# A fused transformer block on one core: mixing weights spread as 8 tokens by 16 heads, a mask product over 128 rows, and half of the base products moved ahead of the map

## The reference

```python
x = x + tanh(g_xattn[0]) * xattn0(ln(x), ctx, mask_b)      # 16 heads of 16, 120 context rows
x = x + tanh(g_ffn[0])   * mix_heads(ln(x))                # mixture-of-heads attention
x = x + tanh(g_xattn[1]) * xattn1(ln(x), ctx, mask_q_by_k) # as xattn0, with an additive mask
x = x + tanh(g_ffn[1])   * moe(ln(x))                      # 12 experts, 3 of them per token

# in mix_heads (16 heads of 64, 8 value experts, 2 chosen per token and head)
mix_v  = sum_k sigmoid(w_k) * one_hot(sel_k)               # b, t, h, e
proj_v = einsum('btc,edc->bted', x, Wv)
v      = einsum('bthe,bted->bhtd', mix_v, proj_v)          # values of each head
# in moe
y = einsum('ebsh,ehd->ebsd', gelu(...), Wdown) + bdown[:, None, None, :]
out = einsum('bse,ebsd->bsd', cw, y)                       # cw: weights of the chosen experts
```

## Time and profile before

| | |
|---|---|
| median of 3 runs | 1486.15 us (1483.16 to 1494.12) |
| the profiled execution | 1487.02 us, span 1485.3 us |
| mean granted clock of PE | 0.906 |
| PE busy | 1296.1 us, 87% |
| DVE busy | 1139.0 us, 77% |
| ACT busy | 902.7 us, 61% |
| POOL busy | 277.7 us, 19% |
| layer 0 | about 75 to 297 us |
| ffn | about 299 to 793 us |
| layer 1 | about 797 to 1024 us |
| routing, then experts | about 1027 to 1084, to 1485 us |

### The profile page before, as it was taken

One profiled execution on the slowest core, in us unless ns is written; L12 is line 12 of the kernel. 1 busy time (PEld: TensorE's weight loads), 2 busy tenths in 40 slices (PEclk: granted clock), 3 DMA queues, 4 the chain that ended last, 5 costly groups with the idle time before them and its releaser, 6 DMA issues. The chain is left out here.

```text
span 1485.3 us, 35279 instructions
## 1 busy us (share of the span) xinstructions
PE 1296.1 (87%) x13822; PEld 1023.6 (69%) x13822; DVE 1139.0 (77%) x2068; ACT 902.7 (61%) x2071; POOL 277.7 (19%) x242
## 2 busy tenths in 40 slices
PE   3399999859989998999965999996599999999996
PEld 2267776536776776776753677765478988999896
DVE  2667775668999999999853577777768888888884
ACT  1267675425766776776751676765257677776773
POOL 2000000010000000000000000000116675666763
PEclk9998785678999999999975899997579999999998
DMA  8000000013335335335410000000568788888871
GB/s 224 12 9 5 5 5 2 1 39 93 97 94 132 96 86 137 97 91 130 120 54 20 9 5 9 2 2 1 187 220 245 229 250 228 244 240 230 243 197 29
DMA packets 172065, 152.96 MB, mean 103 GB/s; under 512 B 62589, under 2 KB 154386, under 8 KB 171906
## 3 DMA queue, kind: packets, MB, share of 16 engines
q1 hardware_dynamic: 151906, 129.51, 29.4%
q0 software_dynamic: 13936, 16.79, 5.9%
q10 hardware_dynamic: 6064, 4.46, 1.1%
HBM read 116.89 MB, written 36.70 MB: 103 GB/s over the span
## 5 line engine op out<-in xcount | busy, mean ns | idle before, releaser
L1850 POOL DMA_INDIRECT out<-m_yo,m_xg x70 | 161.8, 2311 | 129.4 <-DVE m_yo L1965 113.1
L1872 ACT ACTIVATE m_hf<-m_ps,m_bue 128x256 f32<-128x256 f32 x280 | 117.1, 470 | 106.6 <-PE m_ps L84 106.6
L82 PE MATMUL m_ps<-m_xt,m_us 128*128 128x256 f16 x560 | 153.5, 274 | 0.0
L83 PE MATMUL m_ps<-m_xt,m_us 128*128 128x256 f16 x560 | 153.5, 274 | 0.0
L84 PE MATMUL m_ps<-m_xt,m_us 128*128 128x256 f16 x560 | 153.5, 274 | 0.0
L82 PE MATMUL m_ps<-m_ds,m_hs 128*128 128x256 f16 x560 | 152.7, 273 | 0.3 <-DVE m_yo L1965 0.3
L84 PE MATMUL m_ps<-m_ds,m_hs 128*128 128x256 f16 x560 | 152.7, 273 | 0.0
L83 PE MATMUL m_ps<-m_ds,m_hs 128*128 128x256 f16 x560 | 152.7, 273 | 0.0
L1052 ACT ACTIVATE f_pr<-f_ps,f_nb 128x256 f32<-128x256 f32 x256 | 107.6, 476 | 65.9 <-DVE f_nb L1330 65.6
L480 ACT ACTIVATE x_pt<-x_ps 120x512 f16<-120x512 f32 x128 | 76.8, 600 | 116.2 <-PE x_ps L84 108.8
L472 ACT ACTIVATE x_pr<-x_ps,x_mx 128x120 f32<-128x120 f32 x512 | 142.7, 373 | 7.5 <-DVE x_mx L686 7.2
(11 more groups left out here) (367 smaller groups left out, 3893.5 us busy)
## 6 DMA issues: line engine op xcount, KB each, us to landing
m_uraw<-in_L_ffn_Wup SPq DMA_DIRECT2D x35, 1024.0 KB, 6.1
m_draw<-in_L_ffn_Wdown SPq DMA_DIRECT2D x35, 1024.0 KB
head_values<-f_v_row SPq DMA_DIRECT2D x16, 520.0 KB, 5.7
f_vh<-head_values SPq DMA_DIRECT2D x16, 520.0 KB, 4.1
head_outputs<-f_at_row SPq DMA_DIRECT2D x16, 512.0 KB, 2.9
f_at_in_t<-head_outputs SPq DMA_DIRECT2D x16, 512.0 KB, 5.9
expert_values<-f_pv_row SPq DMA_DIRECT2D x8, 512.0 KB, 2.8
f_pv_in_t<-expert_values SPq DMA_DIRECT2D x8, 512.0 KB, 5.6
```

Source lines behind the costliest of these rows:

```text
L82: pe.matmul(out, lhs[0], rhs[0], start=(n == 0), stop=False)
L83: pe.matmul(out, lhs[0], rhs[1], start=False, stop=False)
L1850: pool.indirect_dma_start(rows_of, bass.IndirectOffsetOnAxis(xg[j % RING][:, ti, D:D + 1].bitcast(I32), 0), yo[j % 2][:, ti, :], None, bou ...
L1872: ins = act.activation(hf[:, q, m, :], U(q)[:, m, :], ACT.Gelu, bias=weights.bue[par][:, 2 * q + m:2 * q + m + 1], scale=UNSPLIT)
```

## The change

Three edits. In setup and cross-attention `mask_w` has its value in row 0 of 128 only, and the mask product takes all 128 rows; `e16` takes the whole scale in that one row. In ffn the value product is 8 tokens by 16 heads: 64 rows for each half of the tokens, one product per half group instead of two per group; the spreading makes 2 instructions per batch instead of 4, and the runs that go out to HBM are one head long instead of two. In routing four of the eight groups of base products stand ahead of the map, with other banks.

```diff
-            chain(dve.tensor_scalar(s.row[:], s.row[:], ROWS32 - 1, None, ALU.bitwise_and))
+            chain(dve.tensor_scalar(s.row[:], s.row[:], P - 1, None, ALU.bitwise_and))
-            dve.tensor_scalar(s.e16[:], s.first[:].to_broadcast([P, P]), SPLIT / 4, None, ALU.mult)
+            dve.tensor_scalar(s.e16[:], s.first[:].to_broadcast([P, P]), SPLIT, None, ALU.mult)
...
-                pe.matmul(S(u), s.mask_w[rows, layer, :], bcast_mid(mb[par][rows, :], HG), start=first, stop=False)
+                pe.matmul(S(u), s.mask_w[:, layer, :], bcast_mid(mb[par][:], HG), start=first, stop=False)
...
-SPREAD = 4
+HALF = TG // 2
-        same = sb("same", [P, TG, H8], F16)
+        same = sb("same", [P, HALF, H], F16)
-        mix_in_t = sb("mix_in_t", [P, GROUPS, 4, H8], F16)
-        spread_v = two("spread_v", [P, SPREAD, 4, TG, H8], F16)
+        mix_in_t = sb("mix_in_t", [P, GROUPS, 2, H], F16)
+        spread_v = two("spread_v", [P, GT, 2, HALF, H], F16)
...
-                sp.dma_start(v_d[ti * P:ti * P + P].rearrange("(g t) (h x) c -> (t h) g (x c)", t=TG, x=2),
-                             v_row[:, tiles].rearrange("p g x c -> p g (x c)")).then_inc(v_out[ti], 16)
+                sp.dma_start(v_d[ti * P:ti * P + P].rearrange("(g t) h c -> (t h) g c", t=HALF),
+                             v_row[:, tiles].rearrange("p g j c -> p (g j) c")).then_inc(v_out[ti], 16)
...
-            chain(pool.tensor_copy(same[:], bcast(same_t[:], H8)))
+            chain(pool.tensor_tensor(same[:], bcast(same_t[:, 0:HALF], H), bcast(same_t[:, HALF:TG], H), ALU.add))
...
-                    pe.wait_ge(v_spread, SPREAD * b + r + 1)
+                    pe.wait_ge(v_spread, TPB * b + r // 2 + 1)
...
-                    for n in range(2 * SPREAD):
-                        gl, x = n // 2, n % 2
-                        last = matmul3(pe, front[:, n * DH:(n + 1) * DH],
-                                       [(tuple(spread_v[r % 2][:, gl, 2 * hl + x].rearrange("p t h -> p (t h)") for hl in range(2)),
-                                         tuple(pv_in_t[:, SPREAD * r + gl, hl * DH:hl * DH + DH] for hl in range(2)))])
+                    half = slice(DH * (r % 2), DH * (r % 2) + DH)
+                    for gl in range(GT):
+                        last = matmul3(pe, front[:, gl * DH:(gl + 1) * DH],
+                                       [(tuple(spread_v[r // 2][half, gl, hl].rearrange("p t h -> p (t h)") for hl in range(2)),
+                                         tuple(pv_in_t[half, GT * (r // 2) + gl, hl * DH:hl * DH + DH] for hl in range(2)))])
...
-            def spread_values(b, r):
+            def spread_values(b, ti):
...
-                n = SPREAD * 4
-                dve.tensor_tensor(spread_v[r % 2][:].rearrange("p g l t h -> p (g l) t h"),
+                n = GT * 2
+                dve.tensor_tensor(spread_v[ti][:].rearrange("p g l t h -> p (g l) t h"),
...
-VALUE_STEPS = [10, 11, 12, 13]
+VALUE_STEPS = [10, 12]
...
+BASE_BANKS = (0, 1, 2, 5, 3, 4, 0, 1)
+BASE_AHEAD = 4
...
+            def base_part(q):
+                pe.wait_ge(cwt_done, 3 if q == 3 else q // 2 + 1)
+                if BASE_BANKS[q] in BASE_BANKS[:q]:
+                    pe.wait_ge(b_done, BASE_BANKS.index(BASE_BANKS[q]) + 1)
+                for ti in range(TPB):
+                    tile = TPB * q + ti
+                    last = pe.matmul(BASE(q)[:, ti, :], cwt[:, tile * P:(tile + 1) * P], s.bdown[:], start=True, stop=True)
+                last.then_inc(b_ready, 1)
...
+            for q in range(BASE_AHEAD):
+                base_part(q)
             for n in range(CHOICES):
                 if n % TILES == 0:
                     pe.wait_ge(hot_ready, n // TILES + 1)
                 last = pe.matmul(MAP, lane_hot[:, n, :], column_hot[:, n, :], start=(n == 0), stop=(n == CHOICES - 1))
             last.then_inc(map_ready, 1)
...
+            for q in range(BASE_AHEAD, B):
+                base_part(q)
```

More of the change, by code:

```diff
@@ L886, in parts_of @@
                 return kt[b % 2][:, 0, 2 * r:2 * r + 2, :], kt[b % 2][:, 1, 2 * r:2 * r + 2, :], UNSPLIT / DH ** 0.5
-            rows = v_row[:, SPREAD * r:SPREAD * r + SPREAD].rearrange("p g x c -> p (g x) c")
+            rows = v_row[:, GT * (r // 2):GT * (r // 2) + GT, r % 2, :]
             return rows[:, :, 0:DH], rows[:, :, VW:VW + DH], 1.0 / SPLIT
@@ L924, in mixes_back @@
                 if b >= 1:
-                    sp.wait_ge(v_spread, SPREAD * b)
+                    sp.wait_ge(v_spread, TPB * b)
                 sp.dma_start(mix_in_t[:].rearrange("p g l h -> p g (l h)"),
@@ L1133, in times_v @@
                 pe.wait_ge(pt_done, H * b + h + 1)
-                row = 2 * at_head(h)[0] + at_head(h)[1]
                 for ti in range(TPB):
@@ L1137, in times_v @@
                                    [(tuple(pt[h % 2][:, hl, c, ti, :] for hl in range(2)),
-                                     tuple(vh[b % 2][:, c, row, hl * VW:hl * VW + VW] for hl in range(2))) for c in range(TPB)])
+                                     tuple(vh[b % 2][:, c, h, hl * VW:hl * VW + VW] for hl in range(2))) for c in range(TPB)])
                 last.then_inc(pv_done, 1)
@@ L1292, in normalised_x @@
                 ins.then_inc(xn_ready, 1)
-            def spread_values(b, r):
-                if r == 0:
+            def spread_values(b, ti):
+                if ti == 0:
                     dve.wait_ge(mix_in, 16 * (b + 1))
[L1298 to L1301, removed]
-                n = SPREAD * 4
-                dve.tensor_tensor(spread_v[r % 2][:].rearrange("p g l t h -> p (g l) t h"),
-                                  mix_in_t[:, SPREAD * r:SPREAD * r + SPREAD].rearrange("p g l h -> p (g l) h")
-                                  .unsqueeze(2).to_broadcast([P, n, TG, H8]),
-                                  same[:].unsqueeze(1).to_broadcast([P, n, TG, H8]), ALU.mult).then_inc(v_spread, 1)
+                if b >= 1:
+                    dve.wait_ge(front_ready, USE[b - 1, (F_MIXV, 2 * ti + 1)] + 1)
+                n = GT * 2
+                dve.tensor_tensor(spread_v[ti][:].rearrange("p g l t h -> p (g l) t h"),
+                                  mix_in_t[:, GT * ti:GT * ti + GT].rearrange("p g l h -> p (g l) h")
+                                  .unsqueeze(2).to_broadcast([P, n, HALF, H]),
+                                  same[:].unsqueeze(1).to_broadcast([P, n, HALF, H]), ALU.mult).then_inc(v_spread, 1)
             def spread_masks(b, ti):
@@ L1589, in route @@
         MAP = ps[:, 7, 0:COLUMNS]
-        BASE = lambda q: ps[:, q % 4, :].rearrange("p (t d) -> p t d", t=TPB)
+        BASE = lambda q: ps[:, BASE_BANKS[q], :].rearrange("p (t d) -> p t d", t=TPB)
         block = prep.enter_context(nc.Block())
```

## The result

| | before | after |
|---|---|---|
| median of 20 runs each, timed together | 1483.75 us | 1488.65 us |
| the profiled execution | 1487.02 us | 1487.25 us |
| its span | 1485.3 us | 1485.5 us |

The ratio is 1.0039, interval 1.002 to 1.0058: 0.4% slower, where I forecast 1449 us, 2.5% faster. The two profiled executions end together, but the time inside moved a lot.

The account below looks back on a forecast made before the run. Layer 0 was taken as bound by PE at a switching clock, ffn by DVE and PE in turn, experts by PE; 1487.0 - 29 - 3.5 + 1 - 5.5 = 1450.0, median 0.9 lower: 1449 us, range 1437 to 1470.

Parts of the forecast that it names:

- Edit 1: Layer 0: mask product over 128 rows keeps PE's clock up most times; 29 us saved, bounds 0 and 47.
- Rivals 1 and 4: Clock doesn't follow rows: 1478 us, chance 0.10; clock holds in about half of the places: 1464 us, chance 0.14.
- Edit 2, the gain: ffn: fewer spreadings remove PE's wait at the value products, about 0.5 us per batch, 7 batches: -3.5 us.
- Rival 3: ffn was held by DVE after all: full 2.4 us per batch, 13.5 us more gained, 1436 us; chance 0.06.
- Edit 2, the transport: ffn: 260 B writes of values cost +0.5 us per transfer, two in series; +1 us in all.
- my upper bound: ffn transport: a 260 B packet costs as much as a 520 B one; +2.5 us per batch, +18 in all.
- 0.7 of slack: ffn: values land about 0.7 us before PE uses them, absorbing part of the slower transport.
- head start: ffn: earlier spreading lets the first value write go out sooner; with slack, 1.2 us off the transport's cost.
- Rival 2: ffn: each 260 B packet takes twice a 520 B one; 10 us per batch, +70, 1518 us; slower, chance 0.03.
- Ending within 1% by this mechanism: 260 B writes in ffn cost enough to end between forecast and slower, within 1% of before; chance 0.03.
- Edit 3: Routing: base products fill PE's gap before the map, so the experts' block opens sooner; -5.5 us, bounds -4 and -7.
- The sum: Whole kernel: 1487.0 - 29 - 3.5 + 1 - 5.5 = 1450.0 us, with 0.9 off for the median: 1449 us.

Follow-up runs that it names:

- edit 1 alone: The kernel before with only the mask product over 128 rows changed: 1456.81 us, ratio 0.9813 to before.
- 320 B: The kernel after with each head's run padded with zeros from 260 to 320 B, in SBUF and HBM: 1452.46 us, ratio 0.9793 to before.
- edit 3 alone: The kernel before with only four base groups moved ahead of the map in routing: 1482.90 us, ratio 1.0002 to before.

## Why the prediction was wrong, step by step

**What bounds the kernel.** Right: layer 0 by PE's clock, the slots around the values by PE; ffn at 54.87 us per batch once the values are in time.

**Edit 1.** Right in what it does to the clock, and in size. Forecast 111.5 us for batches 1 to 5, measured 111.60; 22.3 for batch 6, measured 22.30; 4.5 back in the last, measured 5.1. 33.4 was the sum if it always holds, and I took 29 because I expected some falls to stay. With edit 1 alone one of six batches still fell; medians say 27.6. Luck helped: the 12.2 us of batch 6 belonged in part to the profiled execution, since another one of the same code had 24.9 us there (and 29.0 in two batches where this one had 25.4 and 25.8). Rivals 1 and 4 fell.

**Edit 2, the gain.** Forecast 0.5 us per batch, for the one wait of PE and not DVE's 2.4 us: measured 0.70 with 320 B. Rival 3 fell. The number is right in part by luck: the wait of 0.43 us gave back half, about 0.2, and at least another 0.4 is PE's own work, which I had put at nothing.

**Edit 2, the transport: the step that failed.** The term "+1 us in all" measured 35 to 36: 1488.65 against 1452.46 us for the same kernel with 320 B runs, and 34.6 us between ffn's first score maxima and layer 1 in their traces. I priced 2048 writes of 260 B by 2048 reads of 256 B, 2.41 us, and gave +0.5 us per transfer; the page has +2.5. The bulk of the packets is as fast as that row said, 19 ns. The tail is what no row of before showed: mean 34.9 ns. It even lies above my upper bound, which took a 260 B packet to cost what a 520 B one does (1.86 us over 1024 packets on 16 engines, 29 ns each). The price came from a row that differed in two things at once, the direction and the length against 32 B. The bound came from a write that differed in its length alone, and was no bound either: a longer packet was the faster one.

The structure around that term was right, and it turned 2.5 us into 30. From the first write's issue to the second read's landing it took 16.5 us before and 20.5 after: +4.0 (the two writes +5.2, the last read -1.0, the handovers between them the rest). Less the 0.7 of slack and the 0.7 of own gain this gives 2.6, and the steady batches lost 2.6 to 3.3. The head start from the sooner spreading was nil: the first write goes out 6.8 us ahead of the next batch before, and 6.5 after. I had also put the slack of one batch on all. In batches 0, 1 and 7 it was nil already: PE stood 1.79, 0.61 and 0.65 us before the values (those of the last batch landed at 730.83 and were used at 730.92). These batches lost 3.6, 5.8 and 5.7 us, and the last of them made eight where I had counted seven. Rival 2 had the place and the kind of the loss, and its own size, 10 us per batch, was too large: a 260 B packet costs 1.2 times a 520 B one, not twice. Ending within 1% by this mechanism had a chance of 0.03. That was the case.

**Edit 3.** The inner steps were right: gap filled, DVE and SP 6 us sooner. The step that failed is "the experts' block opens when all engines are through", with GpSimd taken as through at the end of its last gather's issue, 1078.27 us. Its drain lasted until 1081.7, so at most 2.5 us were there to gain; the copy to the output then came sooner, beside the gathers, and made the drain 2.0 us longer. From the drain's start to the block's end it is 12.1 us before, 11.6 after: forecast -5.5, measured about -0.5 (medians of edit 3 alone: -1.5, not clear of nothing).

**The sum.** -29 - 3.5 + 1 - 5.5 became, from the same kernel's own runs, about -28, -5 (7 times 0.70), +36 and -0.5. These make +2.5; the medians say +4.9. The -5 is the weak one: it is read in the batches, and the kernel with 320 B is 28.2 us under its before where -28, -5 and -0.5 make -33.5.

## What to carry to other kernels

When an edit changes the length of the runs in HBM, price the write by a row with the same direction and the same length, or widen the range to what a serial wait on it would cost; and where the length is no multiple of 32 B, try it padded to one, as 288 and 320 B did here for 260. Where a block ends, read what every engine's queue does until its last drain, not until its last busy row: a transfer that comes sooner beside another engine's gathers can give back what the sooner start brought. A product that could fill more rows at no extra time is worth trying with all of them where the clock falls, if it needs no further change of row mode.

## What the runs showed of the hardware that I had not expected

- Writes of 260 B: median 19 ns, mean 34.9, almost one in three over 28 ns; 256, 288 and 320 B: mean 17.6, 21.8 and 22.1 ns. A packet of 260 B took 1.6 times as long as one of 320 B, and per byte 1.9 times.
- GpSimd's drain at a block's end lasted until 0.3 us after its last gather had landed, in the eight executions whose traces have that landing. That is 3.1 to 3.5 us past that gather's issue in the eight executions without the copy of 2 MB beside it, 4.8 to 5.7 in the six with it.
- The granted clock followed the rows of a single product per unit, at an unchanged duration of that product (median 372 ns with 32 rows, 366 with 128): 0.75 to 0.81 with 32 rows, 0.91 with 64, 0.97 to 1.00 with 128.
- One more change of row mode cost about 90 ns at full clock: 89 ns per unit with one more, 185 with two more and a product of two columns.
